# A graph network's layer kernel: TensorE signals once for what it does in a row

## The reference

```
# L0, per edge: an MLP of the distance gives a filter of 256 numbers
r = silu((rbf(d) * env(d)) @ rbf_w1 + rbf_b1) @ rbf_w2 + rbf_b2        # 64 wide
W = silu(silu(r @ filt_w1 + filt_b1) @ filt_w2 + filt_b2) @ filt_w3 + filt_b3
agg = segment_sum((x[dst] @ node_w + node_b) * W, src)
h   = layernorm(x + agg) * ln_g + ln_b
x   = layernorm(x + h * sigmoid(h @ gate_w + gate_b))
# L1, per edge: weighted means over neighbours, one half of the features each way
fwd = segment_sum(w * x[dst, :128], src) / deg(src)
bwd = segment_sum(w * x[src, 128:], dst) / deg(dst)
out = layernorm(x + concat(fwd, bwd))
```

## Time and profile before

| | |
|---|---|
| median of 3 runs | 6022.33 us (6012.38 to 6031.83) |
| profiled execution, its own time | 6008.27 us |
| its span, first to last instruction | 6006.5 us |
| instructions | 76202 |
| mean granted TensorE clock | 0.781 of full speed |
| TensorE / VectorE / ScalarE / GpSimd busy | 62% / 40% / 27% / 57% |
| edge stage / sum over sources / spreading / last sums | 2750 / 395 / 1240 / 1265 us |

### The profile page before, as it was taken

The page is one execution under the profiler, slowest core; times in us unless marked ns, Lnnn a source line. Parts: engine busy times, 40 slices in busy tenths (PEclk is TensorE's granted clock), DMA queues, the critical chain, the costliest instruction groups (busy, mean ns, idle before and its releaser), DMA issues. The chain is left out here.

```text
span 6006.5 us, 76202 instructions
## 1 busy us (share of the span) xinstructions
PE 3694.8 (62%) x16356; PEld 2677.7 (45%) x16357; DVE 2377.6 (40%) x7105; ACT 1607.1 (27%) x4212; POOL 3415.2 (57%) x3664
## 2 busy tenths in 40 slices
PE   7777777777777777777799833333332444455444
PEld 5444444444444444444588632222222444444443
DVE  5434434344344443334233622221222445555457
ACT  4333333333333333333366611111111000000000
POOL 2455555554555555555576566666666666566665
PEclk9888888888888888888899966656665667777776
DMA  7333333332333333332499311111111333333334
GB/s 217 94 97 98 95 97 101 95 101 90 94 97 95 95 97 100 98 99 91 131 296 295 120 48 43 44 44 45 44 44 44 99 84 85 84 85 84 84 85 90
DMA packets 460154, 590.18 MB, mean 98 GB/s; under 512 B 65457, under 2 KB 380849, under 8 KB 460081
## 3 DMA queue, kind: packets, MB, share of 16 engines
q0 software_dynamic: 128512, 318.04, 17.5%
q1 hardware_dynamic: 331584, 271.50, 15.6%
HBM read 392.61 MB, written 197.07 MB: 98 GB/s over the span
## 5 line engine op out<-in xcount | busy, mean ns | idle before, releaser
L533 POOL DMA_INDIRECT s_rows<-arena,adr x784 | 770.6, 983 | 1118.4 <-issue 1095.7
L978 PE MATMUL ps<-arena,f2s 128*128 128x512 f32 x1568 | 864.3, 702 | 427.5 <-ACT arena L642 335.3
L573 POOL DMA_INDIRECT d_rows<-arena,adr x832 | 809.5, 973 | 501.1 <-issue 243.6
L586 POOL DMA_INDIRECT arena<-x_half,idx x832 | 800.9, 963 | 507.1 <-issue 230.9
L525 POOL DMA_INDIRECT arena<-y_rows,idx x784 | 758.0, 967 | 305.3 <-issue 227.0
L989 PE MATMUL ps<-f3s,arena 128*128 128x256 f32 x3136 | 800.2, 406 | 171.0 <-issue 112.8
L1166 PE MATMUL ps<-arena 128*128 128x128 f32 x1664 | 376.9, 397 | 649.7 <-DVE arena L1559 566.8
L989 PEld LDWEIGHTS ps<-f3s,arena 128*128 128x128 f32 x3136 | 632.5, 204 | 306.7 <-issue 130.0
L978 PEld LDWEIGHTS ps<-arena,f2s 128*128 128x128 f32 x1568 | 349.8, 229 | 854.1 <-issue 472.1
L1328 DVE TENSOR_TENSOR arena<-arena,ps 128x392 f32<-128x392 bf16 x196 | 109.6, 559 | 1448.1 <-remote 1338.1
L1166 PEld LDWEIGHTS ps<-arena 128*128 128x128 f32 x1664 | 325.6, 292 | 692.7 <-issue 691.5
(11 more groups left out here) (217 smaller groups left out, 5073.0 us busy)
## 6 DMA issues: line engine op xcount, KB each, us to landing
arena<-s_rows SPq DMA_DIRECT2D x104, 1048.0 KB, 5.7
arena<-d_rows SPq DMA_DIRECT2D x52, 1040.0 KB
arena<-de_rows SPq DMA_DIRECT2D x392, 128.0 KB
d_rows<-arena,adr POOLq DMA_INDIRECT x832
arena<-x_half,idx POOLq DMA_INDIRECT x832
s_rows<-tpl_s SPq DMA_DIRECT2D x98, 131.0 KB
arena<-y_rows,idx POOLq DMA_INDIRECT x784
s_rows<-arena,adr POOLq DMA_INDIRECT x784
```

The lines of the kernel that those rows point to most:

```text
L533: pool.indirect_dma_start(s_rows, bass.IndirectOffsetOnAxis(ap=adr[b][:, t:t + 1], axis=0), msg[b][:, t, :], None).then_inc(scattered[b], 16)
L573: pool.indirect_dma_start(d_rows, bass.IndirectOffsetOnAxis(ap=adr2[b][:, t:t + 1], axis=0), drow[b][:, t, :], None).then_inc(scattered_d[ ...
L586: pool.indirect_dma_start(gath2[b][:, t, :], None, x1_half, bass.IndirectOffsetOnAxis(ap=idx2[b][:, t:t + 1], axis=0)).then_inc(gathered2[ ...
L978: last = mm(ps[:, 3 + m, :], f2s[:, k, m * P:(m + 1) * P], s2[:, k, :], start=(k == 0), stop=(k == 1))
```

## The change

It keeps every matmul and its order. In the edge stage one semaphore `ahead_mm` takes the place of `l23_mm`, `rank_mm` and `l1_mm`: it is incremented by the last matmul of what `pe_group` does between layer 4 and layer 5. `l4_mm` and `l5_mm` are incremented once a group, by the last matmul. In L1 `back_mm` is incremented once a group by the last matmul of `pe_back`, and `turns_mm` once a turn by the last matmul of `sum_rows`. Whoever waited for one of the old semaphores waits for the new one, with a count that small functions give (`layer23_of`, `spread_of`, `returned_of` and others). So the waits of `silu2`, of `product` and of the radial basis now end with layer 1 of the group after next, the first SiLU of layer 4 and the first messages with the whole layer, `scale_back` with the turn behind its spread, and `sums_back` with the whole turn. `forth_out` waits for the turn in which its block ends (`ends4`, made in setup by three small instructions on VectorE) and not for the tile. SyncE's loop `load_back` has its first eight steps written out instead of two.

```diff
-        hot_done, rank_mm, prod_done, rank_done = sem("hot_done"), sem("rank_mm"), sem("prod_done"), sem("rank_done")
+        hot_done, prod_done, rank_done = sem("hot_done"), sem("prod_done"), sem("rank_done")
         de_in = [sem(f"de_in{b}") for b in range(4)]
         squared, tanh_done, rbf_done, rbf_chain = sem("squared"), sem("tanh_done"), sem("rbf_done"), sem("rbf_chain")
-        l1_mm, l23_mm, l4_mm, l5_mm = sem("l1_mm"), sem("l23_mm"), sem("l4_mm"), sem("l5_mm")
+        ahead_mm, l4_mm, l5_mm = sem("ahead_mm"), sem("l4_mm"), sem("l5_mm")
...
+        def layer1_of(g):
+            return g + 1
+        def ranks_of(g):
+            return g + 1
+        def layer23_of(g):
+            return g + 2
+        def turned_of(g):
+            return g + 1
+        def spread_of(g):
+            return g + 3 if fixed(g) and g < EARLY else g + 4
+        def returned_of(d):
+            return 1 + (d // 2 + 1 if fixed(d) and d < 2 * LEAD else d - LEAD + 1)
...
-                    sp.wait_ge(aggd_mm, 8 * c - 8)
+                    sp.wait_ge(turns_mm, returned_of((CT // GT) * (c - 1) - 1))
                 sp.dma_start(d_buf[b], d_v[:, bass.ds(c * CT, CT), :]).then_inc(d_in[b], 16)
-            loop(sp, load_back, SC, 2, 2, 0)
+            loop(sp, load_back, SC, 2, 8, 0)
...
-                    hold(pool, aggf_mm, GT * g - (RING - 1) * GT + 1)
+                    hold(pool, turns_mm, g - RING + 2)
...
-                act.wait_ge(l1_mm, g + 1)
+                act.wait_ge(ahead_mm, layer1_of(g))
                 A(s1[b % 2], ps[:, 0, 0:GW], ACT.Silu, bias=col[:, 2:3]).then_inc(s1_done, 1)
             def silu2(g):
-                act.wait_ge(l23_mm, g + 1)
+                act.wait_ge(ahead_mm, layer23_of(g))
                 for m in range(2):
                     A(s2[:, m, :].rearrange("p (h e) -> p h e", h=2),
                       ps[:, 1:3, m * GW:(m + 1) * GW], ACT.Silu, bias=b23[:, m:m + 1]).then_inc(s2_done, 1)
             def silu3(g, b, m):
                 if m == 0 and not (fixed(g) and g < 2):
-                    act.wait_ge(l5_mm, 2 * g - 2)
-                act.wait_ge(l4_mm, 2 * g + m + 1)
+                    act.wait_ge(l5_mm, g - 1)
+                if m == 0:
+                    act.wait_ge(l4_mm, g + 1)
...
-                act.wait_ge(turned_mm, g + 1)
-                if not (fixed(g) and g < 4):
-                    act.wait_ge(spread_mm, g - 3)
+                act.wait_ge(back_mm, turned_of(g))
...
-                last_tile = act.value_load(ends[0:1, n:n + 1], min_val=1, max_val=ST + 1)
-                act.wait_ge(aggf_mm, last_tile)
+                last_turn = act.value_load(ends4[0:1, n:n + 1], min_val=1, max_val=G1 + 1)
+                act.wait_ge(turns_mm, last_turn)
...
-                mm(ps[:, 7, 0:GT * NB2], before_b[:, :], cur, start=False, stop=False,
-                   skip_group_check=True).then_inc(rank_mm, 1)
+                return mm(ps[:, 7, 0:GT * NB2], before_b[:, :], cur, start=False, stop=False, skip_group_check=True)
...
-                mm(ps[:, 0, 0:GW], w1d[:, :], rbf[b % 2], start=True, stop=True).then_inc(l1_mm, 1)
+                return mm(ps[:, 0, 0:GW], w1d[:, :], rbf[b % 2], start=True, stop=True)
...
-                last.then_inc(l23_mm, 1)
+                return last
...
-                    last.then_inc(l4_mm, 1)
+                last.then_inc(l4_mm, 1)
...
-                    if t % 2:
-                        last.then_inc(l5_mm, 1)
+                last.then_inc(l5_mm, 1)
...
             def pe_group(g, q, b):
                 layer4(g)
                 if ahead(g, 1):
-                    layer23(g + 1, b + 1)
+                    last = layer23(g + 1, b + 1)
                 if ahead(g, 2):
                     rank_step(g + 2, b)
-                    layer1(g + 2, b)
+                    last = layer1(g + 2, b)
+                if ahead(g, 1):
+                    last.then_inc(ahead_mm, 1)
...
             def pe_back(g, q, b):
-                spread_rows(g, b)
+                last = spread_rows(g, b)
                 if not fixed(g) or g + 3 < G1:
-                    turn(g + 3, b + 3)
+                    last = turn(g + 3, b + 3)
+                last.then_inc(back_mm, 1)
...
-                    mm(forth[:, bass.ds(at[t], HALF)], hot_f[b][:, t, :], gath2[b][:, t, :],
-                       start=False, stop=False, skip_group_check=True).then_inc(aggf_mm, 1)
+                    last = mm(forth[:, bass.ds(at[t], HALF)], hot_f[b][:, t, :], gath2[b][:, t, :],
+                              start=False, stop=False, skip_group_check=True)
+                return last
             def sum_rows(g, q, b):
-                sum_forth(g, q, b)
+                last = sum_forth(g, q, b)
                 if fixed(g) and g < LEAD:
                     for d in (2 * g, 2 * g + 1):
-                        sum_back(d, d // 8, d % 8)
+                        last = sum_back(d, d // 8, d % 8)
                 elif not fixed(g) or g + LEAD < G1:
-                    sum_back(g + LEAD, q + (b + LEAD) // 8, (b + LEAD) % 8)
+                    last = sum_back(g + LEAD, q + (b + LEAD) // 8, (b + LEAD) % 8)
+                last.then_inc(turns_mm, 1)
...
+                    step(V.tensor_scalar(ends4[:, :], start[:, :], float(2 * GT - 1), None, ALU.add))
+                    step(V.tensor_scalar(ends4[:, :], ends4[:, :], GT.bit_length() - 1, None, ALU.logical_shift_right))
+                    step(V.memset(ends4[:, NB - 1:NB], G1 + 1))
...
-                    dve.wait_ge(rank_mm, g)
+                    dve.wait_ge(ahead_mm, ranks_of(g - 1))
...
-                dve.wait_ge(rank_mm, g + 1)
+                dve.wait_ge(ahead_mm, ranks_of(g))
...
-                dve.wait_ge(l5_mm, 2 * g + h + 1)
+                    dve.wait_ge(l5_mm, g + 1)
...
-                dve.wait_ge(spread_mm, g + 1)
+                dve.wait_ge(back_mm, spread_of(g))
...
-                    dve.wait_ge(aggd_mm, 2 * g - 2)
+                    dve.wait_ge(turns_mm, returned_of(g - 2))
...
+                dve.wait_ge(turns_mm, returned_of(g))
                 for t in range(GT):
                     if not (fixed(g) and g == 0 and t == 0):
                         dve.wait_ge(addedd, GT * g + t)
-                    dve.wait_ge(aggd_mm, 2 * g + t // 2 + 1)
```

More of the change, by code:

```diff
@@ L107, in build @@
         ends = sb("ends", [P, NB], i32)
+        ends4 = sb("ends4", [P, NB], i32)
         ntc = sb("ntc", [NB, 2])
@@ L1105, in turn @@
                         ident_b[:, :])
-                last.then_inc(turned_mm, 1)
+                return last
             def spread_rows(g, b):
@@ L1130, in _ @@
                     pe.wait_ge(slot_free, SLOTS + NB)
-                    turn(0, 0)
-                    turn(1, 1)
+                    turn(0, 0).then_inc(back_mm, 1)
+                    turn(1, 1).then_inc(back_mm, 1)
                 pe.wait_ge(x1_set, c - 1)
```

27 lines of the change are left out of this document (13 added, 14 removed).

## The result

| | before | changed |
|---|---|---|
| median (20 runs each, us) | 6017.04 | 5985.10 |
| lowest, highest | 5996.01, 6032.96 | 5956.36, 6034.24 |
| profiled execution | 6008.27 | 5994.01 |

The ratio is **0.9954, with a 95% interval of 0.9936 to 0.9972**: faster, but by some 30 us and not by 500, and outside the forecast range.

A forecast was written before the change was run, and what follows sets the result against it. It took TensorE's increments, queued one by one during GpSimd's indirect DMAs, as the bound: 6008.3 - 300 - 95 - 150 + 20 = 5483, with the median 14 us above the profiled run, 5500 us; range 5050 to 5850 (0.70).

The forecast's parts named there:

- rival (a), "to the floor": All three DMA stages: increments pass as often as GpSimd needs them, 4830 to 5050 us; chance 0.07.
- So the number of increments a group needs is a rate limit, and the change cuts it.: Stages with indirect DMAs: TensorE's increments pass one by one, one in 10 us, so fewer a group means faster.
- -300: Edge stage: four of seven increments a group go, so 14.75 us a group becomes 13.2, over 196 groups.
- -95: Spreading back in L1: two increments a group become one, 6.08 us a group becomes 5.6.
- -150 us: Last sums: six increments a group become one, 6.25 us a group becomes 5.5.
- The sum is 2.0, so the account closes.: Edge stage: free time 1.1 groups, flush 0.7 and passes 0.2 add up to the two groups of a present cycle.
- Hidden, 0: Edge loop: layers 2 and 3 signalled 2.0 us later, with layer 1, cost nothing because TensorE has layer 5 to run.
- +20: Last sums: the first 12 turns pay 20 us, as VectorE's second sum of a pair waits for the whole turn.
- (b), "an increment costs only its own slot": Edge stage and L1: the increments removed save only their own time, 0 to -60 us, so 5960 to 6020; chance 0.08.
- (c), "blocked by time, not by number": DMA stages: the queue opens only in GpSimd's pauses, fewer increments gain nothing and later signals cost, 6260 us; chance 0.07.

The follow-up runs named there:

- probe40: Kernel before, one-hots of the sum over sources all on ScalarE, plus 256 unused indirect gathers by GpSimd there: 6068.53 us, against 6036.9 without the gathers.
- more_incs: Changed kernel with increments of a semaphore nobody waits for on nearly every matmul that had none: 5992.29 us, ratio 0.9996 to before.
- edge_only: Kernel before with only the edge loop's part of the change, three increments a group, L1 as before: 5965.56 us against 5992.18, ratio 0.9929.
- gap4: Changed kernel with a one-column GpSimd memset behind every four indirect DMAs, on a chip that holds nothing up: 4700.40 us, ratio 1.0024 to before.
- gap4_old: Kernel before with a one-column GpSimd memset behind every four indirect DMAs, on a chip that holds nothing up: 4689.19 us, ratio 0.9996.
- half: Changed kernel with layers 4 and 5 on bf16 operands: ratio to before 1.0026 where nothing is held up, 0.9511 where completions are held.
- pause1: Changed kernel with a short waited GpSimd instruction between DMA batches (edge loop, spreading back): ratio to before 1.2036 where nothing is held, 0.9863 where completions are.

## Why the prediction was wrong

The direction was right and so was the reading of where the time lies; the size rested on one step that fell.

- **What bounds the kernel.** Right: TensorE's results are signalled late during runs of indirect DMAs. `probe40` made the lateness where there was none, the pauses took it away, and on a chip without it the kernel before takes 4681 us, 22% less. The forecast's rival (a), "to the floor", had 4830 to 5050 us for a kernel without the hold-up, 150 us and more above that.
- **"So the number of increments a group needs is a rate limit, and the change cuts it."** This is the step that failed. I had five single passes in 50 us of blocked time, each carrying an increment, and took increments to be what queues. The same five passes are what one sees if something else comes out slowly and now and then has an increment on it. `more_incs` tells the two apart: 23 increments a group instead of three, and the wait stays 17.09 us and the pause 10.21. By the times of the increments one passed in 8.8 us of blocked time with seven a group, one in 36 us with three and one in 2.6 us with 23, so there was no rate of increments that a smaller number could use better. All three gains were computed from that step: -300, -95 and -150 us. In the windows above the three stages gain about 0.12, 0.06 and 0.1 us a group, where 1.55, 0.48 and 0.75 were forecast.
- **"The sum is 2.0, so the account closes."** It closed with numbers of my choosing (where a blocked stretch begins, 1.5 passes a run); an account with two free numbers checks nothing.
- **"Hidden, 0"** for the coarser signals of the edge loop held: `edge_only` gained 0.7%, and the edge stages of `gap4` and `gap4_old` agree within 2 us in GpSimd's scatters.
- **"+20" for the last sums** was of the right size: 12 us. With `edge_only` at 0.9929 and this 0.24% the whole comes to 0.9953, and 0.9954 was measured; the two figures are from chips of different kinds, so the sum is an estimate.
- **The rivals.** (b), "an increment costs only its own slot", gave 5960 to 6020 us and had 0.08: the measured time lies in it, and that increments are cheap was right. The Trainium skill, "TensorE: Matmul & The Clock Gate", section "The cost: per-tile semaphore tail", has 26.3 ns for each; the estimate by it was about 5970 us. The change's own gain (30 us over 2032 increments, about 15 ns each) is below that, and `more_incs` has 6 ns or less. A fixed price for each doesn't fit every run, though: `edge_only` took 784 increments away and gained 27 us on its chip by the medians and 42 by the ratio, 34 to 54 ns each, and why the edge part gains that much was not found; the later signals and the joint wait change with it. I had set (b) aside because late increments spoke against it "as the whole cost"; but late increments and cheap increments go together, and that was the case. (c), "blocked by time, not by number", was nearer than my forecast in that fewer increments gain nothing, but increments do pass in blocked time, and it priced the later signals at 250 us, where `edge_only` shows a gain.

What stays open: what in a chip holds completions up (two of the chips used here did not), whether GpSimd's issuing or the transfers do it, how short and how rare a gap in GpSimd's DMAs may be to prevent it, and whether TensorE's time or the number of its matmuls ahead of layer 4 sets how much gets through. Of what ran, only `half` gained much where completions are held (4.9%) and cost little where they are not (0.3%), and it rounds the operands of two layers; `pause1` is faster on one kind of chip and 20% slower on the other. No version that computes with the same precision was shown to beat the kernel before on both; `edge_only`, which gains 0.7% on the first kind, did not run on the second.

## What to carry to other kernels

When increments arrive late, ask first what is in front of them: add increments that nobody waits for, and if the waits keep their length, merging signals can't shorten them. Where an engine's results arrive late only while GpSimd issues indirect DMAs back to back, a gap between batches can be worth more than anything done to the waiting engines, but price it on GpSimd, which pays if nothing was held. And measure a cause that rests on the chip on more than one chip.

## What the runs showed of the hardware

- The same kernel takes 5947 to 6017 us on some chips and 4681 to 4690 us on others, each within 0.5% or so. Where it was looked at, the difference lies in the stages with indirect DMAs from GpSimd (the sum over sources takes 382 and 383 us): a wait of up to 17.3 us for TensorE's results there, and at most 4.0 us on the other kind.
- The instruction that waits for a late result starts 2 to 3 us behind the last DMA of a run: 2.95 us in the changed kernel, 3.05 us in `more_incs` (2022.73 behind 2019.68), 2.08 us in `probe40`.
- While results are held, they still come out now and then: in `more_incs` at gaps close to multiples of 0.71 us, and behind the run 0.04 us apart. How many such steps a matmul takes was not worked out.
- A gap of 1.99 us behind every four DMAs (5 us) kept increments within 1.0 us of their matmuls, although the first results behind a long run take longer than that.
- An increment costs TensorE next to nothing: 20 more for each of 196 edge groups, and 2500 more in L1, came to 25 us in all.
- A GpSimd memset of one column between two indirect DMAs takes 0.12 us and adds none to the whole: 4689.19 us with 800 of them against 4689.99 without, on a chip that holds nothing up.
